# Mask loads in halves of 64 partitions, and penalty loads ahead of the store of the cross keys

## Chip, cores and metric

The kernel runs on one core of one Trainium2 chip. The metric is the device time of one execution in microseconds, the median of several runs. Engines are named as in the profile: PE (TensorE matmul), PEld (its weight loads), DVE (VectorE), ACT (ScalarE), POOL (GpSimd), SP (SyncE, which here only issues transfers).

## What is computed

One decoder layer in float32 on 1,024 tokens of width 128, with 16 heads of width 8, and three residual layer norms. `mask` is 1,024 x 6,404 int32, where 1 keeps a key and 0 hides it; all rows of it are alike in the data.

```python
def attn(x):                      # self attention, one shared key and value head of width 8
    Q = heads(x @ Wq + bq); K = x @ Wk + bk; V = x @ Wv + bv
    return merge(softmax(Q K^T / sqrt(8)) V) @ Wo + bo
def xattn(query, ctx, mask):      # cross attention over 6,404 context rows, 16 heads
    Q, K, V = heads(query @ Wq.T + bq), heads(ctx @ Wk.T + bk), heads(ctx @ Wv.T + bv)
    s = where(mask == 0, -1e9, Q K^T / sqrt(8))
    return merge(softmax(s) V) @ Wo.T + bo
x = layernorm(x + attn(x))
x = layernorm(x + xattn(x, ctx_1024, mask))
x = layernorm(x + ffn(x))         # router picks one of 8 experts, out = (W_e x + b_e) * its probability
```

## The kernel before

Every engine has its program written out by hand, and semaphores order them. The work of PE is a sequence of steps. The first 128 steps (`SELF`) are self attention: a head and half of the tokens is a unit `g` of 8 steps, 16 units (called heads here). Then come 16 units of cross attention with 10 steps each. A step `s` does the score columns (`ST`, keys by queries, then exp on ACT into `prob`), the scores of a later row block (`RT`, queries by keys, 16 steps ahead: `LEAD`), whose maxima DVE takes (`mxs` and `mxc`), and the product of an earlier `prob` with the values (`O`). Row 128, the first of cross attention (L1732, `RT<-Kr,Qs`), is thus computed in step 112, while self attention's unit 14 is in its first step.

**The maxima.** For unit G, DVE folds the row maxima (`finx`, L929), POOL splits them into a high and a low part (`split_max`, L564 and L566), PE turns them (L1481, at step 8G - 5 in self attention), ACT copies the turned rows (`mxr`, L1238), and SP sends them into four rows of the query stack (`max_rows`, `Qs<-mxr`, 8 KB). The first column step of unit G waits for that copy (`have_max`).

**The mask.** The kernel counts on the chip which key chunks any query may see. POOL loads the mask in 16 pieces of 128 rows and half the (padded) columns, 3,328 int32 each, into two buffers (`load_mask`, L541), turns each into bytes (L611) and adds it up (L617). These loads and counts are interleaved in POOL's program with the splits of the maxima: `MAX_AHEAD` and `MAX_BETWEEN` say which split stands before or within which piece (piece 9: unit 7, piece 12: unit 9, piece 14: unit 10, the last before that piece's own count). `load_mask(m + 2)` stands at the end of piece m. A load also waits until the copy of maxima of unit (m - 2) * 3 // 4 has landed. After the last piece the counts go to PE and DVE, which decide which chunks are kept ("steered").

**The penalty.** Keys that the mask hides get a large negative number through two extra rows (34 and 65, `PENROWS`) of the key stacks `Kr` (for rows) and `Kc` (for columns). POOL makes these numbers (`penr`, `pen_made`), SP stores them to DRAM (`pd`, five pieces, `pen_out`) at unit 13, and loads them into both stacks (`pen_in`) at unit 14. PE waits for `pen_in` at its first cross row, and POOL has cleaned the stacks (`k_clean`) long before.

**The chunk.** `more_keys` on SP waits for `steered`, reads from `steer` how many extra chunks of 256 keys there are (one, in this data), and for each waits for DVE (`mk_done`, L1007) and stores four pieces of its keys to `kd`. POOL waits for those (`kd_more`) before it loads the chunk's part of the stacks (`load_rows(0, 2)`, `load_cols(0, 1)`) and splits the maxima of unit 15. SP's program is one queue in order of writing: what stands behind `more_keys` waits for it.

Of the kernel before, what the change touches and what calls it, by code (L numbers as in the profile page):

```python
# [16 lines left out]
P = 128  # L17
# [17 lines left out]
HALFT = KPAD // 2  # L35
# [8 lines left out]
RU = 10  # L44
SRU = 8
LEAD = 16
SLOTS = 5
E = 8
EPS = 1e-5
# [44 lines left out]
def row_kind(r):  # L94
    return "mrow" if r >= SELF and (r - SELF) % RU >= SRU else "rt"
# [5 lines left out]

rt_order = [(("row", r), "rt") for r in range(LEAD)]
st_order = []
for s_ in range(STEPS + 1):
    if s_ + LEAD < ROWS:
        rt_order.append((("row", s_ + LEAD), row_kind(s_ + LEAD)))
    rt_order += [(n_, "mk" if n_ == "km" else "rt") for n_ in RT_JOBS.get(s_, ())]
# [28 lines left out]
def decoder_layer(nc, t, out):  # L136
    ctx = ExitStack()
    with ctx:
# [42 lines left out]
        vst = sb("vst", [P, NBLK, 2, VW])  # L181
        prob = sb("prob", [P, SLOTS, Q])
        Vs = sb("Vs", [P, QT, VW])
# [29 lines left out]
        maskI = [big[:, k * HALFT:(k + 1) * HALFT] for k in range(2)]  # L213
# [55 lines left out]
        def S(name):  # L269
            return sems[name]  # L270
# [42 lines left out]
        def _(sp):  # L313
# [75 lines left out]
            def more_keys():  # L389

                sp.wait_ge(S("steered"), 1)
                n1 = sp.snap(sp.value_load(steer[0:1, 0:1], min_val=1, max_val=NP))
                with sp.Fori(0, n1) as i:
                    wait_count(sp, S("mk_done"), sp.snap(i + 2))
                    for b in range(4):
                        sp.dma_start(kd[:, b * DH:(b + 1) * DH, ds(sp.snap(i * KC + KS), KC)],
                                     (kx_hi[:, KS:KUSE].bitcast(F32), kx_lo[:, KS:KUSE])[b // 2]) \
                            .then_inc(S("kd_more"), 16)
# [11 lines left out]
            for h in range(UNITS):  # L410
                if h:
                    max_rows(h)
                if h >= 2:
                    o_rows(h - 2)
                if h in (1, 2):
                    if h == 1:
                        sp.wait_ge(S("q_out"), 64)
                    queries(4 + 4 * h, 8 + 4 * h, "q_in")
                if h == 1:
                    for n_, b_ in (("wq_x", wq_x), ("wk_x", wk_x), ("wv_x", wv_x)):  # L420
                        load(b_[:, :], t[n_], "in_w")
                    for a, b_ in (("s", wo_s), ("x", wo_x)):
                        for f in range(2):
                            load(b_[64 * f:64 * f + 64, :],
                                 t[f"wo_{a}"].rearrange("(u f d) o -> u f d o", f=2, d=DH)[:, f, :, :], "in_w")
                if h == 2:
                    load(down[:, :], row("countdown").to_broadcast([P, NP]), "in_w")
                    load(bk_x[:, :], column("bk_x"), "in_w")
                    load(bq["x"][:, :], column("bq_x"), "in_w")
                    for f in range(2):  # L430
                        load(bv_x[64 * f:64 * f + 64, :],
                             t["bv_x"].rearrange("(u f d o) -> u f d o", f=2, d=DH, o=1)[:, f, :, :], "in_w")
                if h == 3:
                    load(wr[:, :], t["wr"], "in_w")
                    load(br[:, :], row("br").to_broadcast([P, E]), "in_w")
                    load(be[:, :], t["be"], "in_w")
                if h == 4:
                    load(ctxn[:, :], t["ctxT"][:, KPAD - KS:KPAD], "ctx_in")
                if h in (6, 7, 8):
                    if h == 6:  # L440
                        sp.wait_ge(S("rt_free"), number(RT_AT, "k"))
                    for b in ((0,), (1, 2), (3,))[h - 6]:
                        load(kd[:, b * DH:(b + 1) * DH, 0:KS],
                             (khi.bitcast(F32), kz)[b // 2], "kd_out")
                if h == 9:
                    o_back("s", 0, 8)
                if h == 12:
                    store_x_queries(0)
                    gather_x_queries(0)
                if h == 13:  # L450
                    sp.wait_ge(S("pen_made"), 1)
                    for k, c in enumerate((*range(CHUNKS - 4, CHUNKS), CHUNKS - 5)):
                        load(pd[:, k * KC:(k + 1) * KC], penr[32 * (c % 4) + c // 4:32 * (c % 4) + c // 4 + 1, :], "pen_out")
                if h == 14:
                    more_keys()
                    sp.wait_ge(S("pen_out"), 16 * 5)
                    sp.wait_ge(S("k_clean"), 2)
                    for k_ in (Kr, Kc):
                        load(k_[PENROWS[0]:PENROWS[1] + 1:PENROWS[1] - PENROWS[0], :].bitcast(F32),
                             pd.to_broadcast([2, KUSE]), "pen_in")  # L460

            o_rows(UNITS - 2)
            max_rows(UNITS)
# [35 lines left out]
        def _(pool):  # L499
# [32 lines left out]
            def load_mask(m):  # L532
                q, w = m // 2, m % 2
                if m >= 2:
                    h = (m - 2) * 3 // 4
                    pool.wait_ge(S("mask_used"), m - 1)
                    if h:
                        pool.wait_ge(S(f"max_in{h % 2}"), 16 * (h // 2 + 1))
                    else:
                        pool.wait_ge(S("q_in"), 16 * 4)  # L540
                pool.dma_start(maskI[m % 2], t["mask"][q * P:(q + 1) * P, w * HALFT:(w + 1) * HALFT]) \  # L541
                    .then_inc(S(f"mask_in{m % 2}"), 16)

            def stack(o, hi, z, sign, name):
                step(g_.tensor_scalar(hi, hi.bitcast(F32), sign, None, ALU.mult))
# [57 lines left out]
            for m in range(2 * QT):  # L603
                q, w = m // 2, m % 2
                if m in MAX_AHEAD:
                    split_max(MAX_AHEAD[m])
                sums = acc8[:, w * HALFT:(w + 1) * HALFT]
                pool.wait_ge(S(f"mask_in{m % 2}"), 16 * (m // 2 + 1))
                if m >= 3:
                    pool.wait_ge(S("mask_added"), m)  # L610
                g_.tensor_scalar(sums if q == 0 else dead8, maskI[m % 2].bitcast(U32), 1.0, 0.0, ALU.min, ALU.max) \  # L611
                    .then_inc(S("mask_used"), 1)
                if m in MAX_BETWEEN:
                    split_max(MAX_BETWEEN[m])
                if q:
                    pool.wait_ge(S("mask_used"), m + 1)
                    g_.tensor_tensor(sums.bitcast(I32), sums.bitcast(I32), dead8.bitcast(I32), ALU.add) \  # L617
                        .then_inc(S("mask_added"), 1)
                else:
                    pool.sem_inc(S("mask_added"), 1)  # L620
                if m + 2 < 2 * QT:
                    load_mask(m + 2)
                if m in (3, 4):
                    pool.wait_ge(S("parts_known"), 1)
                    g_.tensor_copy((Kr, Kc)[m - 3][:, :], rowk[:, 2:3].to_broadcast([P, KUSE])).then_inc(S("k_clean"), 1)
                if m == 5:
                    for f in range(2):
                        g_.tensor_copy(sel[:, :, f, :, :], ident[0:64, 0:64].rearrange("p (u f j) -> p j f u", f=2, j=4)
                                       [:, :, f, :].unsqueeze(3).to_broadcast([64, 4, 8, DH])).then_inc(S("sel_made"), 1)
                if m == 6:  # L630
                    pool.wait_ge(S("in_bo"), 48)
                    add_bias(bo["s"][:, :], slice(0, QT))
                if m == 7:
                    pool.wait_ge(S("in_w"), 16 * 15)
                    g_.tensor_copy(bv_wide[:, :], bv_x[:, :].to_broadcast([P, P])).then_inc(S("bias_tile"), 1)
                if m == 13:
                    pool.wait_ge(S("q_out"), 64)
                    pool.wait_ge(S("kd_out"), 64)
                    g_.tensor_copy(Vx[:, :, :, DH:VW], real[:, :].unsqueeze(2).unsqueeze(3).to_broadcast([P, NB, HEADS, 1])) \
                        .then_inc(S("vx_ones"), 1)  # L640
# [205 lines left out]
        def _(dve):  # L846
# [280 lines left out]
            n1 = None  # L1127
            for s in range(-LEAD, STEPS):
                r = s + LEAD
                if s == KV:  # L1130
# [85 lines left out]
        def _(act):  # L1216
# [62 lines left out]
            def more_columns(j):  # L1279

                before = act.snap(n1 * j)
                with act.Fori(0, n1) as i:
                    done = act.snap(before + i)
                    for k in range(2 * CBLK):
                        b, f = SBLK + k // 2, k % 2
                        s = X(j, b)
                        if f == 0:
                            act.wait_ge(S("pv"), PV[s - SLOTS])
                            wait_count(act, S("mpv"), act.snap(done * CBLK + (k // 2 + 1)))
# [127 lines left out]
        def _(pe):  # L1417
# [253 lines left out]

            for r in range(LEAD):
                if r == SELF_U:
# [282 lines left out]
```

## Time and profile before

| | |
|---|---|
| median of 3 runs | 466.97 us (466.77 to 467.68) |
| the profiled execution | 469.97 us |
| its span, first to last instruction | 467.7 us |
| mean granted clock of TensorE | 0.974 of full speed |
| PE busy | 440.9 us (94%) |
| DVE / ACT / POOL busy | 396.7 (85%) / 358.4 (77%) / 245.1 us (52%) |
| moved by transfers | 56.07 MB, mean 120 GB/s |

The share of busy time is a mean over stages. Self attention lasts from the start to about 205 us, cross attention to about 420, and the feed-forward part is the tail. The mask is loaded from 10 to about 140 us. An engine that is idle in a stage costs something only if another waits for it there. Transfers issued by SP and by POOL stand in two queues that are served by the same 16 DMA engines.

### The profile page before, as it was taken

The numbers are of one execution on the slowest core, as the hardware profiler recorded it, in microseconds if no ns is written. First come the engines' busy times: TensorE is split into PE (matmuls) and PEld (weight loads), VectorE is DVE, ScalarE is ACT, GpSimd is POOL, SyncE is SP. The second block draws the span as 40 slices with busy tenths as digits, with TensorE's granted clock in tenths as the row PEclk, the third lists the DMA queues.
The fourth block names the chain that finished last, engine by engine and source line by source line (L and its number), as shares of the span: only waits on it lengthen the run. The fifth ranks groups of instructions, "written<-read, shape, count | busy, mean of one in ns | idle before, by whom it ended". The sixth has DMA issues, their size and how long they took to land.

```text
span 467.7 us, 10803 instructions
## 1 busy us (share of the span) xinstructions
PE 440.9 (94%) x3885; PEld 176.7 (38%) x3887; DVE 396.7 (85%) x522; ACT 358.4 (77%) x704; POOL 245.1 (52%) x381
## 2 busy tenths in 40 slices
PE   8999999999899999799999999999999999999983
PEld 2433333333334443233343334333443443333441
DVE  4989999999699689689998999999999999941455
ACT  6328889688677877588968988889868788878723
POOL 4726879976799604122447644444447254320453
PEclk9889999999899999989999999999999999999978
DMA  5849968679680073211232346322212122110000
GB/s 129 322 115 315 283 218 297 264 263 332 228 329 13 3 135 80 65 45 46 84 90 69 101 93 111 92 60 58 88 51 70 39 81 69 47 29 26 5 22 25
DMA packets 24595, 56.07 MB, mean 120 GB/s; under 512 B 6442, under 2 KB 15928, under 8 KB 22492
## 3 DMA queue, kind: packets, MB, share of 16 engines
q0 software_dynamic: 7536, 37.91, 24.6%
q1 hardware_dynamic: 16424, 17.24, 14.1%
q8 instruction: 33, 0.54, 0.5%
q10 hardware_dynamic: 580, 0.20, 0.2%
q14 instruction: 22, 0.18, 0.1%
HBM read 45.60 MB, written 9.18 MB: 117 GB/s over the span
## 4 chain that ended last, share of the span: by engine, by line
PE 76%; DVE 10%; DMA 5%; issue 4%; ACT 2%; POOL 2%; POOLq 0%; DVEq 0%; ACTq 0%
PE O L1503 29%; PE ST L1739 15%; PE ST L1530 9%; PE RT L1732 7%; DVE mxs L935 6%; DMA Qs<-mxr 5%; PE RT L1518 4%; PE RT L1625 2%; PE ST L1632 2%; PE RT L1429 1%; PE O L1481 1%; ACT prob L1302 1%; PE RT L1587 1%; PE RT L1595 1%; DVE mxc L952 1%
## 5 line engine op out<-in xcount | busy, mean ns | idle before, releaser
L1302 ACT ACTIVATE prob<-ST 128x512 f32<-128x512 f32 x512 | 279.5, 599 | 59.0 <-PE ST L1530 29.3
L935 DVE TENSOR_REDUCE mxs<-RT 128x2 f32<-128x1024 f32 x128 | 153.0, 1222 | 14.6 <-PE RT L1518 13.5
L952 DVE TENSOR_REDUCE mxc<-RT 128x2 f32<-128x1024 f32 x128 | 152.8, 1221 | 5.8 <-PE RT L1732 5.4
L1739 PE MATMUL ST<-Qs,Kc 64*128 64x512 f32 x320 | 117.4, 450 | 0.0
L1732 PE MATMUL RT<-Kr,Qs 64*128 64x512 f32 (+1 forms) x384 | 114.4, 400 | 2.1 <-issue 2.1
L1503 PE MATMUL O<-prob,vst 128*9 128x256 f32 x1280 | 99.1, 381 | 1.7 <-ACT prob L1291 0.5
L1530 PE MATMUL ST<-Qs,Kself 64*128 64x512 f32 x256 | 96.7, 449 | 4.0 <-DMA Qs<-mxr 3.8
L1518 PE MATMUL RT<-Kself,Qs 64*128 64x512 f32 x256 | 89.3, 465 | 2.2 <-DVE Kself L912 0.9
L681 POOL DMA_DIRECT2D Kr<-kd x96 | 47.8, 502 | 75.9 <-PE RT L1732 60.8
L1503 PE MATMUL O<-prob,Vs 128*9 128x256 f32 x1024 | 81.0, 388 | 1.2 <-ACT osb L1246 0.3
L1739 PEld LDWEIGHTS ST<-Qs,Kc 64*128 64x128 f32 x320 | 50.5, 184 | 65.8 <-issue 38.7
L1530 PEld LDWEIGHTS ST<-Qs,Kself 64*128 64x128 f32 x256 | 39.6, 186 | 55.9 <-ACT prob L1302 38.2
L1732 PEld LDWEIGHTS RT<-Kr,Qs 64*128 64x128 f32 x384 | 51.4, 185 | 2.8 <-issue 2.3
L611 POOL TENSOR_SCALAR big<-big 128x3328 uint8<-128x3328 uint32 x16 | 47.4, 2961 | 4.3 <-DMA big<-in_mask 3.9
L691 POOL DMA_DIRECT2D Kc<-kd x64 | 31.6, 497 | 33.9 <-PE ST L1739 31.6
L953 DVE TENSOR_REDUCE mxc<-RT 128x4 f32<-128x1024 f32 x32 | 38.9, 1223 | 4.8 <-PE RT L1732 4.6
L1503 PEld LDWEIGHTS O<-prob,vst 128*9 128x9 f32 x1280 | 19.4, 88 | 53.0 <-ACT prob L1302 16.2
L1518 PEld LDWEIGHTS RT<-Kself,Qs 64*128 64x128 f32 x256 | 35.3, 188 | 10.8 <-DVE mxs L935 5.0
L1291 ACT ACTIVATE prob<-ST 128x512 f32<-128x512 f32 x64 | 34.7, 595 | 5.2 <-PE ST L1739 3.6
L1503 PEld LDWEIGHTS O<-prob,Vs 128*9 128x9 f32 x1024 | 15.8, 88 | 48.1 <-ACT prob L1302 30.2
L617 POOL TENSOR_TENSOR big<-big 128x832 int32<-128x832 int32 x14 | 27.4, 1960 | 0.8
L564 POOL CAST mxh<-finx 128x8 fp32r<-128x8 f32 x32 | 6.1, 191 | 40.5 <-DVE finx L929 40.3
(219 smaller groups left out, 327.4 us busy)
## 6 DMA issues: line engine op xcount, KB each, us to landing
big<-in_mask POOLq DMA_DIRECT2D x16, 1664.0 KB, 7.3
Kc<-kd POOLq DMA_DIRECT2D x64, 80.0 KB, 2.2
Kr<-kd POOLq DMA_DIRECT2D x64, 64.0 KB, 2.1
od_s<-osb SPq DMA_DIRECT2D x16, 128.0 KB, 2.5
kd<-Vx SPq DMA_DIRECT2D x4, 512.0 KB, 6.9
Qs<-qd_x SPq DMA_DIRECT2D x8, 256.0 KB
od_x<-osb SPq DMA_DIRECT2D x14, 128.0 KB, 1.7
Qs<-qd_s SPq DMA_DIRECT2D x12, 128.0 KB, 5.9
```

The lines of the kernel that those rows point to most:

```text
L611: g_.tensor_scalar(sums if q == 0 else dead8, maskI[m % 2].bitcast(U32), 1.0, 0.0, ALU.min, ALU.max) \
L681: pool.dma_start(Kr[r:r + PROD, w].bitcast(F32), head_rows(U, f)[:, w]).then_inc(S(f"kr{part}"), 16)
L935: freed(v.tensor_reduce(mxs[:, h % 2, c2, :].rearrange("p (f t) -> p f t", f=2)[:, :, q], bank[:, :].rearrange("p (f k) -> p f k", f=2), A ...
L952: return v.tensor_reduce(o[:, :, u % 4], src, AX.X, ALU.max)
L953: return v.tensor_reduce(o[:, :, 2 * (u - SRU):2 * (u - SRU) + 2], src.rearrange("p f (t k) -> p f t k", t=2), AX.X, ALU.max)
L1291: nc.scalar.activation(prob[:, s % SLOTS, f * HALF:(f + 1) * HALF], ST[ST_AT[s, f][2]][:, :], ACT.Exp) \
L1302: freed(nc.scalar.activation(prob[:, s % SLOTS, f * HALF:(f + 1) * HALF], bank[:, :], ACT.Exp))
L1503: mm = mmul(O[32 * q:32 * q + VW, 0:256], v[q // 2], prob[:, slot, q * 256:(q + 1) * 256], start=G is not None, stop=False, skip_group_che ...
L1518: mm = mmul(bank[:, f * HALF:(f + 1) * HALF], Qs[STACK[f], h, q * P:(q + 1) * P], Kself[STACK[f], c2 * 512:(c2 + 1) * 512], start=True, st ...
L1530: st_done(mmul(st_place((c, f))[:, :], Kself[STACK[f], b * P:(b + 1) * P], Qs[STACK[f], g, :], start=True, stop=True))
L1732: mm = mmul(o_, Qs[STACK[f], U, q * P:(q + 1) * P], Kr[STACK[f], w], start=True, stop=not gen, skip_group_check=True)
L1739: mm = mmul(o[:, :], Kc[STACK[f], b * P:(b + 1) * P], Qs[STACK[f], j, :], start=True, stop=not gen, skip_group_check=True)
```

## The change

`load_mask` issues two transfers of 64 partitions in place of one of 128, one after the other on POOL's queue and counted on the same semaphore, and POOL waits for the count of both. On SP, at unit 14, the wait for `pen_out` and `k_clean` and the two penalty loads into `Kr` and `Kc` now stand before `more_keys` instead of behind it; in what `pen_in` means for PE nothing changes.

```diff
+MPART = 64
...
                 if h == 14:
-                    more_keys()
                     sp.wait_ge(S("pen_out"), 16 * 5)
                     sp.wait_ge(S("k_clean"), 2)
                     for k_ in (Kr, Kc):
                         load(k_[PENROWS[0]:PENROWS[1] + 1:PENROWS[1] - PENROWS[0], :].bitcast(F32),
                              pd.to_broadcast([2, KUSE]), "pen_in")
+                if h == 14:
+                    more_keys()
...
-                pool.dma_start(maskI[m % 2], t["mask"][q * P:(q + 1) * P, w * HALFT:(w + 1) * HALFT]) \
-                    .then_inc(S(f"mask_in{m % 2}"), 16)
+                for p0 in range(0, P, MPART):
+                    pool.dma_start(maskI[m % 2][p0:p0 + MPART, :],
+                                   t["mask"][q * P + p0:q * P + p0 + MPART, w * HALFT:(w + 1) * HALFT]) \
+                        .then_inc(S(f"mask_in{m % 2}"), 16)
...
-                pool.wait_ge(S(f"mask_in{m % 2}"), 16 * (m // 2 + 1))
+                pool.wait_ge(S(f"mask_in{m % 2}"), 16 * P // MPART * (m // 2 + 1))
```

## Rows read from the trace of the kernel before

**Rows 1.** The page, part 1: busy time, share, instructions of each engine.
```profile
PE 440.9 (94%) x3885; PEld 176.7 (38%) x3887; DVE 396.7 (85%) x522; ACT 358.4 (77%) x704; POOL 245.1 (52%) x381
```
**Rows 2.** Waits: who waited for whom, us in total, times, longest.
```profile
PE ST L1530 <- DMA Qs<-mxr: 3.8, 3, 2.6
...
PE O L1481 <- POOL mxh L566: 0.8, 1, 0.8
```
**Rows 3.** The chain of waits, 80 to 215 us: start, us, what.
```profile
110.56 8.32 DMA Qs<-mxr
...
124.24 0.59 ACT prob L1302
125.02 1.80 DMA Qs<-mxr
...
127.38 0.60 POOL big L541
...
132.98 0.57 POOL big L541
...
182.70 0.42 PE ST L1530
...
186.68 0.44 PE ST L1530
...
195.22 0.42 PE ST L1530
195.64 2.06 issue
...
203.05 0.43 PE ST L1530
```
**Rows 4.** Timeline of SP's issues, 165 to 212 us.
```profile
187.72 0.44 SPq L315 DMA_DIRECT2D od_s<-osb  x1
191.72 2.92 SPq L396 DMA_DIRECT2D kd<-big  x4
194.95 0.70 SPq L315 DMA_DIRECT2D Kr<-pd  x1
195.71 0.60 SPq L315 DMA_DIRECT2D Kc<-pd  x1
```
**Rows 5.** Waits of SP's queue.
```profile
SPq L296 <- DVE big L1007: 2.2, 1, 2.2
```
**Rows 6.** Timeline of all engines, 193.5 to 204 us; in brackets idle time before.
```profile
196.66 0.98 POOL L681 DMA_DIRECT2D Kr<-kd  x2 [11.15 <-DMA kd<-big]
...
199.07 0.20 POOL L566 TENSOR_TENSOR mxh<-finx,mxh 128x8 fp32r<-128x8 f32 x1
...
202.67 0.38 PE L1481 MATMUL O<-ident,mxh 128*16 128x128 f32 x2
```
**Rows 7.** Windows: length, busy us by engine, then PEclk, DMA share, GB/s.
```profile
194.60:198.00 3.40, 1.34 (x13) 0.59 (x12) 1.55 (x3) 1.55 (x3) 1.34 (x3) 1.00 0.32 88
198.00:201.40 3.40, 3.40 (x23) 0.75 (x20) 1.79 (x2) 2.00 (x4) 1.22 (x5) 0.50 0.20 63
```
**Rows 8.** Timeline of POOL, 0 to 172 us.
```profile
95.35 0.58 POOL L541 DMA_DIRECT2D big<-in_mask  x1 [1.69 <-DMA Qs<-mxr]
...
109.62 0.60 POOL L541 DMA_DIRECT2D big<-in_mask  x1
...
119.45 0.57 POOL L541 DMA_DIRECT2D big<-in_mask  x1 [0.84 <-DMA Qs<-mxr]
...
123.25 0.20 POOL L566 TENSOR_TENSOR mxh<-finx,mxh 128x8 fp32r<-128x8 f32 x1
```
**Rows 9.** POOL's issues by tile and line: ns min/median/max.
```profile
L541 POOL DMA_DIRECT2D big<-in_mask x16: 556/593/812, 9.8 to 133.0; - x16
...
L681 POOL DMA_DIRECT2D Kr<-kd x96: 496/496/615, 181.5 to 398.6; - x96
```
**Rows 10.** The page, part 6: KB each, median us from issue to landing.
```profile
Kr<-kd POOLq DMA_DIRECT2D x64, 64.0 KB, 2.1
```

More of the change, by code:

```diff
@@ L453, in _ @@
                         load(pd[:, k * KC:(k + 1) * KC], penr[32 * (c % 4) + c // 4:32 * (c % 4) + c // 4 + 1, :], "pen_out")
-                if h == 14:
-                    more_keys()
                     sp.wait_ge(S("pen_out"), 16 * 5)
```

## Prediction

> **What bounds the kernel now.** The page's busy shares come first. TensorE (PE) is busy 94% of the span, VectorE (DVE) 85%, GpSimd (POOL) 52% [rows 1]. So PE's queue sets the end, and a change that touches only POOL, SP and transfers can act only where PE stands idle for one of them. The list of waits says where that is before the profile's last stage. PE loses 3.8 us in three waits to the copy of the row maxima into the query stacks, the longest 2.6 us, and 0.8 us in one wait to POOL's split of the maxima [rows 2]. The chain of waits puts these in order of time and adds a third kind, a piece called "issue" of 2.06 us at 195.64 [rows 3]: PE waited, and the profile names nobody. I read the rest around these places, since the two edits sit on them: the mask loads share the transfers with the maxima copies and POOL with the splits, and the penalty loads are the last thing that SP issues before PE goes on at 197.70.
>
> **Part two first: the penalty loads ahead of more_keys.** SP's timeline has, at head 14, the store of the outputs at 187.72, then four stores of cross keys from 191.72 for 2.92 us, and only then the two penalty loads at 194.95 and 195.71 [rows 4]. Between 188.2 and 191.5 SP reads the chunk count and waits 2.2 us for DVE's cross keys [rows 5]. What the penalty loads need, the rows of pd, was sent off long before. PE's first cross row, L1732, waits for both loads (`pen_in`, 32). The second is issued by 196.3 (195.71 and 0.60), and PE's wait ends at 197.7, some 1.4 us behind; a transfer of POOL's of this kind and small size lands in 2.1 us from its issue [rows 10], so the two times belong together. That is my reading of the unnamed wait.
>
> After the change SP issues the two loads at about 188.2. They take 0.70 + 0.60 and so some 1.4 us with the gap, which comes out of the 2.2 us that SP waits for DVE anyway. The four key stores still start at 191.72, with 0.8 us to spare, so nothing queued behind them on SP is later. Were that cover gone, the key stores and POOL's chunk loads would be 1.4 us later. The penalty rows land near 191, 4 us before PE asks for them.
>
> The gain is more than the 2.06 us. The column step of ST at 195.22 and the one at 203.05 are the first and fourth step of their head, 7.83 us apart; the same two steps of the head before, at 182.70 and 186.68, are 3.98 us apart [rows 3]. So the place costs 3.85 us. The windows say what the other 1.8 us are: PE is busy 1.34 of 3.40 us around the wait, and in the next 3.40 us its granted clock is 0.50, that is 1.2 GHz instead of 2.4 [rows 7]. Without the idle stretch I expect the clock to stay at 1.00 there, as it does in the heads ahead.
>
> What is late next? The turn of the maxima for head 15, on PE at 202.67, needs POOL's split. POOL had waited 11.15 us for the key stores to land, issued four chunk loads from 196.66, and ended the split at 199.07 + 0.20 = 199.27 [rows 6]. None of this moves, since the key stores don't. A PE that is 3.85 us earlier would reach the turn at 198.8 and wait for POOL until 199.3. So the gain is cut to 202.67 - 199.27 = 3.4 us. Bounds: 2.06, if only the wait goes, and 3.85. I take 3.4.
>
> **Part one: the mask loads in two halves.** Nothing is computed otherwise and no byte is added. Removed are 16 loads of 128 partitions, added 32 of 64, and the count that POOL waits for doubles with them. On POOL's queue a 128-partition load occupies 0.593 us in the median, and a load of 32 partitions (Kr) 0.496 [rows 9]. The trace has none of 64. A straight line between the two gives 0.528, so a pair takes 1.06 and a mask load costs POOL 0.46 us more, 7.4 us over all 16. Bounds: none, if the second issue is hidden; and 1.03 each, if a half costs 0.812, the dearest mask load. I take the straight line, because the two medians are of the same queue and near each other.
>
> Most of the 7.4 us falls into POOL's own idle time. From the load of piece 6 on POOL works with hardly a pause, so four loads (pieces 6 to 9), 4 x 0.46 = 1.8 us, have piled up when it comes to the load at 95.35; there it sat idle 1.69 us for a copy of maxima [rows 8]. Were that cover gone, the splits of heads 7 and 8 would be late. Before the load at 119.45 it idled 0.84 us, and one load's 0.46 fits in. The split behind it ends at 123.45, and PE's turn hangs on ACT's work from 124.24 instead [rows 3], so another 0.46 fits as well. But then the chain runs through POOL: the copy of 125.02 lands, POOL issues the load of 127.38, counts, issues the load of 132.98, and only then splits the maxima of head 10, for which PE waits [rows 2, 3]. Two loads lie in this piece, so 2 x 0.46 = 0.93 us go on the path (0 to 2.06 by the bounds).
>
> And the transfers? The chain has the copy of 110.56 under way 8.32 us; the one of 125.02, with no mask load ahead of it, takes 1.80 [rows 3]. So a copy of maxima issued just behind a mask load does lie behind its bytes. The load ahead of the copy of 110.56 was issued at 109.62 [rows 8], 0.94 us before. After the change its second half comes 0.53 us after the first, still ahead of the copy, and the same bytes are in front. I take 0 for this. Bounds: a gain of all 3.8 us of rows 2, or a loss if each half paid a start of its own, 2.1 us, the landing of the smallest loads of this queue. The nearest row is the copy behind a whole mask load, whose bytes stay.
> The Trainium skill's page "DMA: Bandwidth & Descriptors", section Rules for kernel authors, says not to split a transfer into disjoint partition halves, since both halves use the same 16 engines and serialize. By that rule the transfers bring nothing and the second issue is pure cost, as in my sum; nothing in it is needed for the numbers here.
>
> **Sum.** -3.4 + 0.93 = -2.5 us. The profiled execution took 469.97 us with a span of 467.7, so it would be 467.5 with a span of 465.2. The median of the runs is 466.97, 3.0 below the profiled one; the same difference on it gives 464.5.
>
> **Rivals.**
> A. The clock falls all the same, because PE's pieces around the head change keep it too little busy. Then the wait alone goes: -2.06 + 0.93 = -1.1, 465.8. Against it: only half a microsecond of waiting is left there, and for the clock the rows speak of a stretch in which PE was busy 40%.
> B. The halves let the copies of maxima in between. The two short waits (1.2 us together) vanish. At head 8 the gain is cut: POOL, free 0.84 us sooner but with 0.46 more to issue, ends the split at 123.1 in place of 123.45, and PE's turn moves from 124.3 to there, 1.2 us. Together -2.5 - 2.4 = -4.9, 462.1. For it: it needs only that a half is passed on as a unit. Against it: the second half is issued before the copy.
> The page "DMA: Bandwidth & Descriptors", section Queues, rings and completion order, of the Trainium skill says that an engine changes between queues only at packet boundaries, a packet being 9 to 17 descriptors. Smaller loads would then make smaller packets, which is this rival; no view here shows packets by engine.
> C. POOL pays 0.812 per half: the path gets 2.06, net -1.3, 465.6.
> D. The unnamed wait is for something else than the penalty rows. Then only the 0.93 remains: 467.9. Against it: SP's times fit too well.
> E, the other side: slower. Each half pays its own start, so that a mask load stays in the way for up to 2.1 us longer. The copies for which PE waits already (heads 1, 3 and 8) land that much later, 3 x 2.1 = +6.3, net +3.8, 470.8. It decides from 0.8 us per copy on, where 3 x 0.8 eats the 2.5. For it: the bytes of a small load take far less than its 2.1 us. Against it: the two halves are issued 0.53 us apart, so the second one's start passes while the first one's bytes move.
>
> **How the numbers follow.** Forecast 0.52, A 0.12, B 0.13, C 0.08, D 0.05, E 0.10. What a measurement of this kernel can tell from no change is 0.2%, 0.93 us, so faster means under 466.0. The forecast, B, and nearly all of A and C lie there: 0.79. D is near the edge and goes to same with the slow ends of A and C: 0.09. E and a part of D are slower: 0.12. The likeliest case has a range of its own from 463.5 to 465.8 (the bounds of POOL's cost and of the clock). With B and with both costs at their upper bounds (-2.06 + 2.06 = 0) it becomes 461.8 to 467.1.
>
> **What the profile after would show.** Right: SP issues the penalty loads near 188.2 and the key stores still at 191.7 against their surroundings; the 2.06 us piece is gone and PE waits up to half a microsecond for POOL's split at the turn for head 15; the clock after it is 1.00; the four steps take about 4.4 us; POOL has 32 mask loads of 0.53; the wait for POOL before head 10 grows from 0.8 to 1.7. Wrong: a wait of PE at its first cross row; key stores later than DVE's cross keys; a copy of maxima behind a mask load that lands clearly earlier or later than 8.3 us after its issue. Beyond that, the tail has stretches at the lower clock of its own, and if they move, so does the sum.

## The result: 8% slower

The changed kernel takes 505.24 us (median of 4 runs, 504.86 to 506.45), the kernel before 467.33 beside it. The ratio is 1.0815, with a 95% interval of 1.079 to 1.084. The forecast was 464.5 us, a gain. One of the ten executions of e5 below (612.43 us, with a mean granted clock of 0.556) is in a slow state that the others are not in, and is left out of its median.

The profiled execution of after took 504.96 us with a span of 503.2, so 35.5 us more of span than before. Its page, parts 1 and 2, and the mask's issue row of part 6 (KB each, median us to landing):

```profile
span 503.2 us, 10821 instructions
PE 449.8 (89%) x3887; PEld 177.7 (35%) x3887; DVE 396.8 (79%) x522; ACT 359.1 (71%) x704; POOL 252.9 (50%) x397
...
PEclk9888869999895989999999999999999999999988
DMA  4967996999998920642123125542220222211000
...
big<-in_mask POOLq DMA_DIRECT2D x32, 832.0 KB, 10.9
```

The mask's issue row on the page of before:

```profile
big<-in_mask POOLq DMA_DIRECT2D x16, 1664.0 KB, 7.3
```

Against [rows 1], DVE does the same work in the same time (396.8 us), and PE is busy 8.9 us longer, because its clock is at the lower level in a part of the first 15 slices. All the new idle time lies there too. The mask's row matters most: a half carries 832 KB and lands 10.9 us after its issue in the median, where a whole load of 1,664 KB took 7.3. (A half may have to wait for the one before it, so the two figures are no rates yet; e1 below has those.)

The list of waits of after, whole span, the rows that answer to [rows 2], with the one for POOL's wait for the mask:

```profile
POOL big L614 <- DMA big<-in_mask: 30.7, 11, 5.4
...
PE ST L1533 <- DMA Qs<-mxr: 24.4, 7, 7.1
...
PE O L1484 <- POOL mxh L569: 8.0, 3, 6.8
```

PE's waits for the copies of maxima grew from 3.8 to 24.4 us, those for POOL's split from 0.8 to 8.0. That is 27.8 us more; with the 8.9 us by which PE is busy longer it makes 36.7, close to what was lost before the stage's end (39.1 us, below). The chain of waits of after, 0 to 215 us, now goes through transfers:

```profile
42.10 9.38 DMA Qs<-mxr
...
57.23 12.79 DMA Qs<-mxr
...
76.78 7.89 DMA Qs<-mxr
...
114.21 10.31 DMA big<-in_mask
...
130.13 13.19 DMA big<-in_mask
...
166.63 14.58 DMA big<-in_mask
```

The mask's own landing is on the path three times, where before it was not there at all: [rows 3] is an excerpt, and in the whole chain of before from 0 to 215 us the only transfers are four copies of maxima. Windows over the time in which the mask is loaded, of before and then of after (busy us by engine; then PEclk, DMA share, GB/s):

```profile
10.00:146.00 136.00, 128.26 (x1086) 48.02 (x1085) 124.59 (x128) 97.70 (x193) 103.30 (x83) 0.96 0.75 257
```

```profile
10.00:181.00 171.00, 136.01 (x1075) 49.29 (x1071) 124.85 (x129) 97.79 (x191) 106.36 (x95) 0.88 0.91 204
```

The DMA engines are held more (0.91 of the time against 0.75) and move less (204 GB/s against 257). So they aren't idle: each byte takes them longer. The last piece of the mask is turned into bytes at 181.3 us, where before it was at 140.7 (POOL's L614 and L611), 40.6 us later.

TensorE's clock fell behind the long waits. The step of 70.06, on which PE had waited 7.1 us for a copy of maxima, and the work behind it up to 73.5 ran at a granted clock of 0.50, that is 1.2 GHz; from 77.0 to 80.0 it stood at 1.00 again.

The penalty loads, on the other hand, brought what was forecast, though SP issues them earlier than the forecast has it. SP's timeline of after:

```profile
219.02 1.44 SPq L316 DMA_DIRECT2D pd<-big  x5
221.33 0.63 SPq L316 DMA_DIRECT2D Kr<-pd  x1
222.01 0.57 SPq L316 DMA_DIRECT2D Kc<-pd  x1
...
226.85 0.45 SPq L316 DMA_DIRECT2D od_s<-osb  x1
...
230.86 2.97 SPq L397 DMA_DIRECT2D kd<-big  x4
```

The loads stand right behind the stores to `pd`, in unit 13. The line `if h == 14:` moved down together with `more_keys()` (its diff is under e2), so what was left behind belongs to `if h == 13:`. The sentence and the excerpt of the diff ahead of the prediction, which have the two loads at unit 14, are wrong in this.

Chain of waits of after, 214 to 250 us, and the timeline of PE (its first cross row is now L1735):

```profile
238.07 0.21 POOL mxh L569
238.32 0.39 PE O L1484 x2
238.72 0.42 PE ST L1533
```

```profile
234.28 0.49 PE L1533 MATMUL ST<-Qs,Kself 64*128 64x512 f32 x1
234.28 0.72 PE L1735 MATMUL RT<-Kr,Qs 64*128 64x512 f32 x2
...
238.32 0.39 PE L1484 MATMUL O<-ident,mxh 128*16 128x128 f32 x2 [0.19 <-POOL mxh L569]
238.65 0.49 PE L1533 MATMUL ST<-Qs,Kself 64*128 64x512 f32 x1
```

The first cross row starts with no idle time before it. The column steps that were 7.83 us apart in [rows 3] start 4.37 us apart (234.28 and 238.65). On the time axis the step of 203.05 now stands at 238.72, 35.7 us later, which is the difference in span (35.5) to 0.2 us. So the part up to the head's first step lost 39.1 us (35.7 + 3.46) and the penalty loads gave 3.46 back.

### The profile page after: what moved, and what is told of

The parts are those of the page before. It is cut to its first block, busy times and chain, and to the rows that moved or that the text cites. A ratio compares the mean times of both kernels' runs of the same rounds, so it can differ in the third digit from the quotient of the medians.

```text
span 503.2 us, 10821 instructions
## 1 busy us (share of the span) xinstructions
PE 449.8 (89%) x3887; PEld 177.7 (35%) x3887; DVE 396.8 (79%) x522; ACT 359.1 (71%) x704; POOL 252.9 (50%) x397
## 4 chain that ended last, share of the span: by engine, by line
PE 57%; DMA 17%; POOL 10%; DVE 7%; issue 5%; ACT 2%; SPq 1%; POOLq 0%; DVEq 0%; ACTq 0%
PE O L1506 21%; PE ST L1742 14%; DMA big<-in_mask 8%; DMA Qs<-mxr 7%; PE RT L1735 7%; POOL big L614 4%; PE ST L1533 4%; DVE mxs L938 3%; DMA qd_s<-Vx 2%; POOL big L620 2%; PE RT L1628 2%; PE RT L1521 1%; PE ST L1635 1%; PE RT L1432 1%; PE O L1484 1%
## 5 line engine op out<-in xcount | busy, mean ns | idle before, releaser
L1533 PE MATMUL ST<-Qs,Kself 64*128 64x512 f32 x256 | 102.3, 476 | 24.6 <-DMA Qs<-mxr 24.4
L1735 PE MATMUL RT<-Kr,Qs 64*128 64x512 f32 (+1 forms) x384 | 114.9, 400 | 0.0
L1521 PE MATMUL RT<-Kself,Qs 64*128 64x512 f32 x256 | 96.0, 487 | 2.2 <-DVE Kself L915 0.9
L1506 PE MATMUL O<-prob,Vs 128*9 128x256 f32 x1024 | 84.7, 404 | 1.0 <-ACT osb L1249 0.3
L1742 PEld LDWEIGHTS ST<-Qs,Kc 64*128 64x128 f32 x320 | 50.8, 185 | 66.4 <-issue 39.1
L1533 PEld LDWEIGHTS ST<-Qs,Kself 64*128 64x128 f32 x256 | 42.1, 199 | 81.3 <-ACT prob L1305 42.8
L614 POOL TENSOR_SCALAR big<-big 128x3328 uint8<-128x3328 uint32 x16 | 47.3, 2958 | 30.8 <-DMA big<-in_mask 30.7
L1735 PEld LDWEIGHTS RT<-Kr,Qs 64*128 64x128 f32 x384 | 51.6, 185 | 0.4 <-DVE mxc L955 0.4
L1521 PEld LDWEIGHTS RT<-Kself,Qs 64*128 64x128 f32 x256 | 38.3, 199 | 9.6 <-DVE mxs L938 4.9
L543 POOL DMA_DIRECT2D big<-in_mask x32 | 17.7, 553 | 17.3 <-DMA Qs<-qd_s 8.1
## 6 DMA issues: line engine op xcount, KB each, us to landing
big<-in_mask POOLq DMA_DIRECT2D x32, 832.0 KB, 10.9
```

The source lines that it names most:

```text
L1506: mm = mmul(O[32 * q:32 * q + VW, 0:256], v[q // 2], prob[:, slot, q * 256:(q + 1) * 256], start=G is not None, stop=False, skip_group_che ...
L1521: mm = mmul(bank[:, f * HALF:(f + 1) * HALF], Qs[STACK[f], h, q * P:(q + 1) * P], Kself[STACK[f], c2 * 512:(c2 + 1) * 512], start=True, st ...
L1533: st_done(mmul(st_place((c, f))[:, :], Kself[STACK[f], b * P:(b + 1) * P], Qs[STACK[f], g, :], start=True, stop=True))
L1735: mm = mmul(o_, Qs[STACK[f], U, q * P:(q + 1) * P], Kr[STACK[f], w], start=True, stop=not gen, skip_group_check=True)
L1742: mm = mmul(o[:, :], Kc[STACK[f], b * P:(b + 1) * P], Qs[STACK[f], j, :], start=True, stop=not gen, skip_group_check=True)
```

## Experiments

Two theories stood at the start. **P (partitions):** a load's rate hangs on which partitions it writes, and 0 to 63 or 64 to 127 alone reach half of the write paths. **C (count):** twice as many loads, each with a start and an end of its own, are what costs. This second one was rival E of the prediction.

**e1: loads by themselves.** A kernel that computes nothing of the layer, only loads; one execution, each load three times. A tile's name says where its load goes.

```python
one("full",    (T["full"][:, :], rows))
one("low",     (T["low"][0:64, :], rows[0:64, :]))
one("high",    (T["high"][64:128, :], rows[0:64, :]))
one("middle",  (T["middle"][32:96, :], rows[0:64, :]))
one("evens",   (T["evens"][0:P:2, :], rows[0:64, :]))
one("quarter", (T["quarter"][0:32, :], rows[0:32, :]))
one("pairlow", (T["pairlow"][0:64, :], rows[0:64, :]), (T["pairlow"][64:128, :], rows[64:128, :]))
one("paircol", (T["paircol"][:, 0:W // 2], rows[:, 0:W // 2]), (T["paircol"][:, W // 2:W], rows[:, W // 2:W]))
```

Also "pairmix" (one half to the even partitions, one to the odd ones), and two loads of 64 rows and half the columns from SP's queue, "splow" to partitions 0 to 63 and "spmiddle" to 32 to 95.

> This kernel computes nothing of the layer: it only loads parts of the mask, one load or one pair after the other, each waited for, three times over, into tiles named for what they are, and stores zeros. Theory P (partitions): the rate of a load hangs on which partitions it writes; 0 to 63, or 64 to 127, reach only half of the write paths, 32 to 95 reach all. Theory C (count): what costs is that there are two loads, each with a start and an end of its own, whatever their partitions. Worked out from a whole load's 7.1 us to landing and 2.1 us for a small one (so some 1,664 KB in 4 to 5 us): by P, full 6 to 7 us, low and high (832 KB) as long as full, 6 to 7, middle (32 to 95, same bytes, same source rows) 4 to 4.7, the second of pairlow 10 to 11, of paircol (two column halves of all partitions) 6.5 to 7.5. By C, low, high and middle all 4 to 4.7, and pairlow and paircol alike, 8.5 to 9.5. evens (every second partition) tells whether the spread over time or the set of partitions counts: 4 to 4.7 if only the set does, 6 if neighbouring descriptors still meet on one path.

The issue rows (KB each, median us to landing) and then windows, around full, low, middle, pairlow and paircol in turn:

```profile
full<-in_mask POOLq DMA_DIRECT2D x3, 1664.0 KB, 6.8
...
low<-in_mask POOLq DMA_DIRECT2D x3, 832.0 KB, 6.7
high<-in_mask POOLq DMA_DIRECT2D x3, 832.0 KB, 6.7
middle<-in_mask POOLq DMA_DIRECT2D x3, 832.0 KB, 4.9
evens<-in_mask POOLq DMA_DIRECT2D x3, 832.0 KB, 4.8
quarter<-in_mask POOLq DMA_DIRECT2D x3, 416.0 KB, 4.2
splow<-in_mask SPq DMA_DIRECT2D x3, 416.0 KB, 4.4
spmiddle<-in_mask SPq DMA_DIRECT2D x3, 416.0 KB, 3.6
```

```profile
2.90:8.50 5.60, 0.00 (x0) 1.00 0.87 304
10.30:15.20 4.90, 0.00 (x0) 1.00 0.78 174
...
24.30:27.70 3.40, 0.00 (x0) 1.00 0.77 251
...
38.90:47.60 8.70, 0.00 (x0) 1.00 0.89 196
49.80:55.10 5.30, 0.00 (x0) 1.00 0.90 322
```

This bears out theory P. The low 64 partitions take as long for half the bytes (6.7 us) as all 128 for the whole (6.8). The same 64 source rows sent to partitions 32 to 95 take 4.9. Source, bytes, number of rows and queue are alike in low and middle; only the destination differs. It is the set that counts and not neighbourhood, since evens lands in 4.8. (Both are a little above the 4 to 4.7 us expected.) By theory P quarter and low write the same paths, and from one to the other 416 KB more take 2.5 us more, 170 GB/s. Nor is it that only half of the 16 DMA engines work for low: their mean busy share in its window is 0.78, which 8 of 16 can't give. The landings of the pairs, min/median/max, so the last figure is that of a second half, from its own issue:

```profile
DMA to landing us min/median/max: 6.6/8.3/10.1
```

```profile
DMA to landing us min/median/max: 4.7/5.5/6.2
```

```profile
DMA to landing us min/median/max: 4.6/5.4/6.3
```

First pairlow, then paircol, then pairmix. The second half by columns lands after 6.2 us, the one to the odd partitions after 6.3, the one to partitions 64 to 127 after 10.1. So two things meet in pairlow. Each half is slow by itself, and the second, which goes to the other partitions, doesn't fill the paths that the first leaves free: the pair moves 196 GB/s together, where paircol moves 322.

The Trainium skill's page "SBUF — State Buffer", section Door 1: The DMA port swizzle, says just this: the port is picked by bits 2 to 4 and bit 6 of the partition number, so 0 to 63 reach 8 of 16 ports, no more than 0 to 31, and get 196 GB/s for 1 MiB where 128 partitions get 328. The windows agree in the ratio: 174 against 304 is 0.57, and 196 against 328 is 0.60. Middle agrees too, whose partitions have both values of bit 6. What the runs here show is that the set of partitions sets the rate; none of them tests bits 2 to 4 by themselves.

**e2: the penalty loads alone.** Mask loaded whole.

```diff
                         load(pd[:, k * KC:(k + 1) * KC], penr[32 * (c % 4) + c // 4:32 * (c % 4) + c // 4 + 1, :], "pen_out")
-                if h == 14:
-                    more_keys()
                     sp.wait_ge(S("pen_out"), 16 * 5)
...
                              pd.to_broadcast([2, KUSE]), "pen_in")
+                if h == 14:
+                    more_keys()
```

> Only the penalty loads are moved; the mask is loaded whole. By my prediction's second part the gain is 3.4 us against the kernel before (0.7%, ratio 0.993), with the piece of 2.06 us gone, a granted clock of 1.00 after it and a short wait for the split of head 15. A rival in which the move does nothing without the slower mask loads: ratio 1.000.

Ratio 0.9925, interval 0.989 to 0.996: 464.7 us beside 468.0. The windows of this run around the place, which answer to [rows 7]:

```profile
194.60:198.00 3.40, 3.32 (x36) 1.16 (x28) 3.37 (x5) 3.10 (x7) 1.48 (x3) 1.00 0.27 76
198.00:201.40 3.40, 3.06 (x34) 1.00 (x34) 2.61 (x3) 2.61 (x6) 1.97 (x6) 1.00 0.24 68
```

PE is busy 3.32 us where it was 1.34, and the clock stays at 1.00, 2.4 GHz. SP issues the two loads at 182.00 and 182.67, and the key stores at 191.53.

**e3: the mask halves alone.**

```diff
+                for p0 in range(0, P, MPART):
+                    pool.dma_start(maskI[m % 2][p0:p0 + MPART, :],
...
```

> Only the mask loads are halved by partitions. If the two edits add up, this is 505.2 plus 3.4, so 508 to 509 us, ratio 1.088 to 1.090. If the moved loads had a part in the loss: below 505.

511.66 us, ratio 1.096 (1.089 to 1.104). That is above the expected 1.088 to 1.090, whose upper end the interval just takes in. The edits add up as far as this can tell. The profile of this run has the wait before the first cross row again (2.2 us).

**e4: halves by columns.** Everything as in the changed kernel, but a half is all partitions and half the columns.

```diff
-                for p0 in range(0, P, MPART):
+                for c0 in range(0, HALFT, HALFT // 2):
+                    pool.dma_start(maskI[m % 2][:, c0:c0 + HALFT // 2],
```

> The changed kernel with each mask load in two halves by columns instead of by partitions: as many loads, as many bytes, as many issues on POOL, all 128 partitions in each. Theory P: the loss goes except for POOL's issue time, so 463.5 to 466 us, ratio 0.993 to 0.998, and a median landing near 5 to 7.5 us. Theory C: 500 us or more, ratio above 1.07, as with the halves by partitions.

465.02 us, ratio 0.994 (0.990 to 0.998). The whole loss is gone with as many loads, bytes and issues. Its rows for the loads, its wait for POOL's split, and its window for the mask's stage:

```profile
L543 POOL DMA_DIRECT2D big<-in_mask x32: 527/546/812, 9.6 to 131.0; - x32
...
DMA to landing us min/median/max: 2.3/6.5/11.8
```

```profile
PE O L1484 <- POOL mxh L569: 2.2, 3, 1.2
```

```profile
33.00:146.00 113.00, 107.75 (x1020) 39.44 (x1020) 105.91 (x108) 92.27 (x184) 99.40 (x89) 1.00 0.77 262
```

262 GB/s is what the kernel before moves in the same window. PE's waits for the copies of maxima are 1.2 us here. Theory C has fallen as the cause of the loss.

**e5: every second partition.** The halves by rows stay, 64 contiguous source rows each, but they go to the even and then the odd partitions.

```diff
+                for p0 in range(2):
+                    pool.dma_start(maskI[m % 2][p0:P:2, :],
+                                   t["mask"][q * P + 64 * p0:q * P + 64 * p0 + 64, w * HALFT:(w + 1) * HALFT]) \
```

> The changed kernel, its mask loads still halved by rows (64 source rows each, contiguous), but the first half goes to the even partitions and the second to the odd ones; the sum over rows that the kernel makes of them doesn't care. Number of loads, bytes and source rows are those of the changed kernel, only the destination partitions differ. Theory P (the set of partitions a load writes sets its rate): no loss, ratio 0.990 to 0.999, median landing 5.5 to 7 us. A theory in which the source rows or the count of loads matter: as the changed kernel, ratio 1.08.

466.02 us, ratio 0.9955 (0.992 to 0.999), median landing 6.4 us. So the source side has no part in the loss: only the destination partitions differ from the changed kernel.

**e6: three parts.** 32 to 95, 0 to 31, 96 to 127.

```diff
+                for p0, p1 in ((32, 96), (0, 32), (96, P)):
+                    pool.dma_start(maskI[m % 2][p0:p1, :],
```

> The changed kernel with each mask load in three: partitions 32 to 95 at once, then 0 to 31, then 96 to 127. By theory P the first part runs at the full rate and the other two at half of it, so a piece takes 6 us of transfer where a whole one takes 4 and two halves 8: about half of the loss of 38 us remains, plus 1.0 us of POOL's issue time per piece, so 480 to 495 us, ratio 1.03 to 1.06. By a theory of counts, three loads are worse than two: ratio above 1.08.

488.55 us, ratio 1.044 (1.038 to 1.050). Three loads cost about half of what two cost, as theory P has it: half of the bytes go to partitions 32 to 95. PE's waits for the copies of maxima are 15.4 us, between 3.8 and 24.4.

**e7: half of the pieces.** Pieces 0 to 7 in halves by partitions, 8 to 15 by columns.

```diff
+                    if m < 8:
+                        dst = maskI[m % 2][k * MPART:(k + 1) * MPART, :]
...
+                    else:
+                        c0 = k * HALFT // 2
```

> The changed kernel with pieces 0 to 7 in halves by partitions and pieces 8 to 15 in halves by columns, 32 loads as there. If the loss is the time for which the DMA engines are held (they were busy 76% of the mask's stage before, 94% after), it is in proportion to the slow pieces once the engines are full: half of it or somewhat less, 478 to 488 us, ratio 1.025 to 1.045. If the loss came from one place late in the stage only (the maxima of heads 8 to 11), under 470.

490.61 us, ratio 1.047 (1.040 to 1.054). Counted from the column halves of e4 that is 60% of the loss, just above the range I gave. So the loss isn't made at one place late in the stage, and the pieces 8 to 15 by themselves would bring the other 40%, if the shares add up (no run has them alone). That the early half costs the larger share may have to do with SP's stores and loads of queries, which share the engines there (in after the four stores `qd_s<-Vx` land in 6.9 us, before in 3.1), but this isn't shown.

**e8: an earlier split.** e2, and POOL splits the maxima of head 10 before it writes the ones of the value tensor.

```diff
-MAX_AHEAD = {0: 0, 2: 2, 6: 5, 9: 7, 14: 10}
+MAX_AHEAD = {0: 0, 2: 2, 6: 5, 9: 7}
...
                 if m == 13:
+                    split_max(10)
```

> Mask loaded whole, penalty loads moved, and POOL splits the maxima of head 10 right after it has issued the last mask load, before it writes the ones of the value tensor (1.72 us) in place of after. In the trace of before PE waited 0.8 us for this split. Expected against the kernel with the penalty loads alone: 0.7 us less, so ratio 0.990 to 0.992 to before; if the ones are then late for something, no gain.

462.84 us, ratio 0.988 (0.984 to 0.993), the fastest of all. PE's wait for the split, this run's row:

```profile
PE O L1483 <- POOL mxh L567: 0.8, 2, 0.5
```

In e2 the same wait was 1.4 us in three, 0.75 of it before head 10, and that one is gone here. The gain over e2 (464.7 us, 0.9925) has the expected direction, but by the medians it is 1.9 us where 0.7 was expected, and the two intervals overlap. So neither the gain nor its size is settled.

## Why the prediction was wrong

**The step that failed** is in part one: "the same bytes are in front. I take 0 for this". I costed the halves by their bytes and their number, and took it that 64 partitions get the same rate. They get little more than half of it: 174 GB/s against 304 (e1). In place of 0, the term is the whole loss. By e1's windows a pair takes 8.70 us where a whole load takes 5.60, so an estimate for 16 pieces is 16 x 3.1 = 50 us of transfer time more. The engines were free in a part of the stage, and some 38 us came through. Their busy share rises from 0.75 to 0.91, and the mask is in 40 us later. My own sign of being wrong came up as well: copies of maxima on the chain took up to 12.79 us, not 8.3. My upper bound for the transfers, a start of 2.1 us for each half, was a bound of the wrong thing. No row that I had could warn me, since the loads of the mask's size in that trace all write 128 partitions; the small ones, from which I took the 2.1 us, are too short to show a rate.

The rule that the prediction cites from the Trainium skill's page "DMA: Bandwidth & Descriptors", section Rules for kernel authors, says that partition halves serialize. The pair of e1 agrees: together its halves move 196 GB/s. The runs show more: each half alone takes the time of the whole (6.7 us against 6.8).

**Rival E** had the right side and the right victims, the copies of maxima, but not the mechanism. Two halves that each reach both sides of partition 64 cost next to nothing (465.0 us in e4 and 466.0 in e5, beside 464.7 for whole loads in e2), and its price was 3.8 us net where the runs show 38.

**POOL's issue time** was sized rightly. A half costs 0.526 us in the median of after (0.528 forecast), and POOL's busy time rose by 7.8 us (252.9 against 245.1; 7.4 forecast). That 0.93 us of it goes on the path can't be seen in after, where the transfers rule. In e4 PE waits 2.2 us for POOL's splits, in e2 1.4; the difference of 0.8 is of that size, but it isn't where I put it. Before head 10, where I expected 1.7 us, PE waits 1.24 (e2: 0.75), and before head 9, where I took the 0.46 to fit, it waits 0.82 (e2: 0.31). The times of the two, 465.0 and 464.7, can't tell.

**Rival B**, halves that let the copies in between, isn't borne out. PE's waits for the copies are shorter in e4 (1.2 us) than before (3.8) or in e2 (3.0), but in e5, with as many halves, they are 4.4, so no effect of the halving can be read from them. Its 462.1 us is a ratio of 0.990 to the kernel before, clearly outside the interval of e5 and at the lower edge of that of e4.

**The penalty loads** went by the forecast but for the place of their issue. I had read the change as if SP issued them at 188.2, within its wait for DVE, and so counted on 2.2 us of cover. They stand in unit 13 and go out 6 us earlier (182.00 and 182.67 in e2), so the cover wasn't needed; SP waits 0.8 us there for the stores to `pd` and has nothing else to send until 186.8. The gain doesn't hang on this, since the rows are there long before PE asks for them either way. The rest came as forecast: the unnamed wait was for them (rival D falls), the clock stayed up (rival A falls), the next thing late was POOL's split for head 15 (238.07 + 0.20, the turn at 238.32), and the gain was 3.46 us by the trace against 3.4. By the runs of e2 it is 3.5 us of 468.0, with an interval from 1.9 to 5.1.

## What to carry to other kernels

When a transfer is split, ask first which partitions each part writes. Cut along the free dimension (e4) or into every second partition (e5), and here the split cost 0.3 and 1.3 us beside whole loads (e2), less than the runs can tell apart; cut at partition 64, each part ran at 0.57 of the rate (e1). Partitions 32 to 95 alone are fast as well, but they leave 0 to 31 and 96 to 127, and a split in three cost 4% (e6). The DMA engines' busy share of 0.75 said how little room there was: at 0.57 of the rate the same transfers would want 0.75 / 0.57 = 1.3 of the stage (an estimate that takes them all for loads of the mask), so they couldn't hide. And where the profile calls a wait "issue", as on PE's first cross row, look for the transfer that the instruction's own program waits for, and match its landing with the end of the wait: here e2, where the loads come early, has lost this wait, and e3, where they come late, has it again.

## What was new about the hardware

The same 64 rows of 13,312 bytes, 832 KB, land in 6.7 us at partitions 0 to 63 or 64 to 127 and in 4.9 us at 32 to 95; the 1,664 KB to all 128 take 6.8. From SP's queue it is the same in kind: 416 KB land in 4.4 us at 0 to 63 and in 3.6 at 32 to 95. Loads to 0 to 63 and to 64 to 127, issued one behind the other, don't run side by side: the pair moves 196 GB/s, a pair of column halves 322. TensorE's clock paid as well: in after it stood at 0.88 of full speed on average over the mask's stage, against 0.96 before. Behind PE's wait of 7.1 us it was 0.50, that is 1.2 GHz, for the next 3.5 us.
